# Turning the exponentials of a slots stage in 32x32 blocks on VectorE and through DRAM, where TensorE transposed them

## The chip, the cores and the metric

The kernel runs on one core of a Trainium2 chip. The metric is the device time of one execution in microseconds, from the first to the last instruction of the program. Three runs of the kernel before took 2634.92, 2635.74 and 2637.29 us; their median is 2635.74 us.

## The reference

The kernel computes one transformer layer on float32 data: grouped causal attention with a residual and a layer norm, and then a mixture of experts with soft routing, again with a residual and a layer norm. The change lies in the mixture. Its core, cut to what matters:

```python
x_ln = (x - mean) / jnp.sqrt(var + LN_EPS) * gamma + beta          # B=2, N=2048, D=512
x_n = _l2norm(x_ln, -1) * scale
mu_n = _l2norm(mu, 0)                                              # D, E=16, S=128
logits = jnp.einsum('bnd,des->bnes', x_n, mu_n)
dispatch = jax.nn.softmax(logits, axis=1)                          # over the tokens
combine = jax.nn.softmax(logits.reshape(B, N, E * S), axis=-1)
slot_in = jnp.einsum('bnd,bnes->besd', x_ln, dispatch)
h = jax.nn.gelu(jnp.einsum('besd,edh->besh', slot_in, W1) + b1, approximate=False)
slot_out = jnp.einsum('besh,ehd->besd', h, W2) + b2
out = jnp.einsum('bsd,bns->bnd', slot_out.reshape(B, E * S, D), combine)
```

## The kernel before

The program is a sequence of five stages with a barrier between them: projections, attention, post (output projection and norms), slots, and combine. The change is in slots, which computes `logits`, `slot_in`, `h` and `slot_out`. Every product is made in three passes of float32r halves (`three_passes`, L71 to L75): high times high, high times low, low times high, so each tensor that enters a product is first split, its high half by a copy on ScalarE and its low half by a subtraction on VectorE.

The slots stage works in 32 units, one for each of 2 batches and 16 experts. A unit's logits are a tile of 128 slots by 2048 tokens, held as four groups j = 0 to 3 of 512 tokens (JG = 4), each one PSUM bank. With slots on the partitions the softmax over the tokens is a reduction along the row. The product for `slot_in` however contracts over tokens, so it wants the exponentials with tokens on the partitions: they have to be turned. Per unit:

- **logits(j)** on TensorE (L1347 on): 12 matmuls of 512 columns per group into `ps_l`.
- **copy(j)** on ScalarE (L1469) scales them into `logit`; the SP queue stores all four groups at once to DRAM (`store_logits`, L1313, 1 MB) for the combine stage.
- **maximum(j)** and **largest(j)** on VectorE (L1577, L1593): the row's maximum, whose negative goes into the exponential's bias after the fourth group (L1580, L1582), and a running maximum `most` per token.
- **exp(j)** on ScalarE (L1479) writes `ex`, of which there are two, one for even and one for odd units, and sums the row.
- **transpose(j)** on TensorE (L1371): four 128x128 transposes against an identity into one of two banks of `ps_t`. **split_hi(j)** (ScalarE, L1488) and **split_lo(j)** (VectorE, L1608) make `eT_hi` and `eT_lo` from that bank; of each there are two, for even and odd groups.
- **product(j)** on TensorE: 12 matmuls of 512 columns on `eT_hi`, `eT_lo` and the token rows `xl_hi`, `xl_lo`.
- then, one unit at a time through one bank `ps_e`: **slot_in** (ScalarE, L1497), its transpose (`slot_in_t`, L1396), its split (L1503, L1614), **hidden** (12 matmuls of 128 columns), **gelu** (L1509, L1513), **hidden_lo** (L1618), **slot_out** (3 matmuls), **bias** (L1623), and the split and store of the result (L1519, L1627, L1327, L1329).

The units are pipelined by hand. Each engine has a list of parts with a lag; `walk` runs i from 0 up and emits, in the list's order, each part for unit i minus its lag. So in one round TensorE makes the logits of unit n, the products of unit n-1 and the hidden layer of unit n-2. Engines execute strictly in this written order, and a part that waits for a semaphore holds everything behind it on its engine. TensorE's list:

```python
walk([(1, logits(0)), (3, slot_in_t), (1, logits(1)), (1, logits(2)), (3, hidden),
      (2, transpose(0)), (1, logits(3)), (2, transpose(1)), (3, slot_out), (2, product(0)), (2, transpose(2)),
      (2, product(1)), (2, transpose(3)), (2, product(2)), (1, largest_t), (2, product(3)), (2, largest_rows)])
```

The SP queue issues nearly all DMAs of the stage in one order as well: per round the next expert's `mu` (L1291), the logits (L1313), the expert's weights (L1319, L1320, L1323) and the slot results. Once per batch it loads the token rows: `xT` (L1299) for the logits and `xl` (L1308, 16 tiles) for the products. GpSimd only makes the identity in this stage.

## Time and profile before

| | |
|---|---|
| median of three runs | 2635.74 us |
| the profiled execution, its own time | 2634.77 us |
| its span, first to last instruction | 2633.1 us |
| mean granted TensorE clock | 0.972 of full speed |
| TensorE busy in the span | 2519.9 us (96%) |
| VectorE busy | 1673.7 us (64%) |
| ScalarE busy | 1444.5 us (55%) |
| GpSimd busy | 1099.3 us (42%) |
| slots stage, first to last instruction | about 1352 to 2241 us of the span |
| DMA moved in the whole span | 304.37 MB, 116 GB/s on average |

TensorE is busy nearly throughout. A busy time of matmuls counts them from start to modelled end, and they overlap, so what a matmul costs is read from one start to the next. Idle time of an engine costs nothing unless something that ends last waits for it. The views used below are the page of the profile, its table of instruction groups, the instructions in order of time on one engine, the busy time of each engine in chosen stretches, and the DMA issues with their time from issue to landing.

### The profile page before, as it was taken

What the parts mean: (1) busy time and instruction counts of PE and PEld (TensorE: products, weight loads), DVE (VectorE), ACT (ScalarE), POOL (GpSimd) and SP (SyncE); (2) the same over time, 40 slices, a digit from 0 to 9 for tenths busy, and PEclk for the clock granted to TensorE, in tenths of its full rate; (3) what the DMA queues carried; (4) which work ended last, traced back from release to release, by engine and by line L of the source; (5) the groups of instructions that cost most, each with busy time, mean ns of one, the idle gap of its engine ahead of it and who ended that gap; (6) DMA issues with size and microseconds to landing.
All of it is one profiled execution on the core that took longest, in us unless ns stands there. A gap on an engine that the chain in (4) does not pass through costs nothing. (4 is left out here: it accounts for less than half of the span.)

```text
span 2633.1 us, 39463 instructions
## 1 busy us (share of the span) xinstructions
PE 2519.9 (96%) x13730; PEld 1774.6 (67%) x13730; DVE 1673.7 (64%) x3601; ACT 1444.5 (55%) x2780; POOL 1099.3 (42%) x657
## 2 busy tenths in 40 slices
PE   8989999999999999996969999999999998799998
PEld 7865555555555555544747888887888887688886
DVE  3348887878787877835965444456444444577776
ACT  3214566666566666664865555566555554454453
POOL 4304868677677777686930000000000000355553
PEclk9978999999999999998979999999999999899999
DMA  7841121212221121105963323254232322875453
GB/s 245 283 147 36 35 60 38 63 43 55 53 54 50 49 53 47 34 9 189 350 245 116 120 81 120 81 181 147 86 114 90 111 92 81 288 233 150 132 159 102
DMA packets 205063, 304.37 MB, mean 116 GB/s; under 512 B 40225, under 2 KB 86337, under 8 KB 200641
## 3 DMA queue, kind: packets, MB, share of 16 engines
q1 hardware_dynamic: 201296, 294.72, 35.8%
q0 software_dynamic: 1920, 5.25, 0.6%
q8 instruction: 110, 1.80, 0.3%
q10 hardware_dynamic: 1648, 1.88, 0.2%
q14 instruction: 89, 0.72, 0.1%
HBM read 184.83 MB, written 116.42 MB: 114 GB/s over the span
## 5 line engine op out<-in xcount | busy, mean ns | idle before, releaser
L834 ACT ACTIVATE p_probs<-p_ps_s 128x512 f32<-128x512 f32 (+3 forms) x1280 | 597.0, 539 | 340.4 <-PE p_ps_s L766 330.8
L861 DVE TENSOR_REDUCE p_parts<-p_ps_m 128x1 f32<-128x512 f32 x768 | 472.4, 682 | 91.4 <-PE p_ps_m L753 91.0
L722 POOL TENSOR_TENSOR p_added<-p_added,p_probs 128x2048 f32<-128x2048 f32 x112 | 513.7, 4587 | 20.6 <-ACT p_probs L834 8.4
L753 PE MATMUL p_ps_m<-k_m,q 96*128 96x512 f32 (+3 forms) x1280 | 477.0, 403 | 13.2 <-PEq L1878 7.8
L766 PE MATMUL p_ps_s<-q,k_e 98*128 98x512 f32 (+3 forms) x1280 | 450.6, 382 | 2.2 <-ACT p_probs L834 2.2
L1726 POOL MEMSET p_power<- 128x1 f32 x1 | 0.1, 99 | 890.1 <-POOLq L1878 890.1
L753 PEld LDWEIGHTS p_ps_m<-k_m,q 96*128 96x128 f32 x1280 | 242.7, 193 | 187.8 <-DVE p_parts L861 89.8
L766 PEld LDWEIGHTS p_ps_s<-q,k_e 98*128 98x128 f32 x1280 | 238.3, 191 | 135.2 <-issue 56.7
L785 PE MATMUL p_ps_c<-p_probs,v_e 128*32 128x512 f32 (+3 forms) x2560 | 287.5, 540 | 3.7 <-POOL p_probs L707 3.7
L865 DVE CUSTOM_DVE_ANT_0 p_masked<-p_ps_m,p_mask 128x384 f32<-128x384 f32 (+3 forms) x512 | 223.8, 487 | 99.6 <-PE p_ps_m L753 96.3
L1739 POOL TENSOR_TENSOR p_acc<-p_acc,p_lg 128x512 f32<-128x512 f32 x112 | 162.0, 1447 | 154.6 <-ACT p_lg L1791 151.6
L73 PE MATMUL p_ps_l<-p_xT_hi,p_mu_hi 128*128 128x512 f32 x512 | 207.2, 405 | 16.7 <-DVE p_xT_lo L1555 12.0
L73 PE MATMUL p_ps_o<-p_so,p_c_hi 128*128 128x512 f32 x512 | 204.0, 398 | 17.4 <-DVE p_c_lo L1827 17.4
L73 PE MATMUL p_ps_s<-p_xl_hi,p_eT_hi 128*128 128x512 f32 x512 | 209.2, 409 | 5.5 <-DVE p_eT_lo L1608 5.5
L1469 ACT ACTIVATE p_logit<-p_ps_l,p_inv_n 128x512 f32<-128x512 f32 x128 | 87.8, 688 | 217.1 <-PE p_ps_l L75 217.1
L74 PE MATMUL p_ps_o<-p_so,p_c_hi 128*128 128x512 f32 x512 | 203.2, 397 | 0.0
L75 PE MATMUL p_ps_o<-p_so,p_c_lo 128*128 128x512 f32 x512 | 203.0, 397 | 0.0
L74 PE MATMUL p_ps_s<-p_xl_lo,p_eT_hi 128*128 128x512 f32 x512 | 201.8, 394 | 0.0
L75 PE MATMUL p_ps_s<-p_xl_hi,p_eT_lo 128*128 128x512 f32 x512 | 201.7, 394 | 0.0
L74 PE MATMUL p_ps_l<-p_xT_lo,p_mu_hi 128*128 128x512 f32 x512 | 201.5, 393 | 0.0
L75 PE MATMUL p_ps_l<-p_xT_hi,p_mu_lo 128*128 128x512 f32 x512 | 201.1, 393 | 0.0
L1791 ACT ACTIVATE p_lg<-p_lg 128x512 f32<-128x512 f32 x128 | 81.1, 634 | 170.6 <-DVE p_lg L1823 170.2
(179 smaller groups left out, 4523.7 us busy)
## 6 DMA issues: line engine op xcount, KB each, us to landing
logits_t<-p_logit SPq DMA_DIRECT2D x32, 1024.0 KB, 5.0
p_lg<-logits_t SPq DMA_DIRECT2D x128, 256.0 KB, 3.7
q<-q_t SPq DMA_DIRECT2D x96, 256.0 KB, 4.6
p_w_raw<-L_ffn_W_dram SPq DMA_DIRECT2D x64, 256.0 KB, 5.4
p_so<-slot_out SPq DMA_DIRECT2D x32, 512.0 KB, 6.3
p_x<-L_attn_x_dram SPq DMA_DIRECT2D x32, 256.0 KB, 5.6
q_t<-p_f_hi SPq DMA_DIRECT2D x32, 256.0 KB, 5.3
q_t<-p_f_lo SPq DMA_DIRECT2D x32, 256.0 KB, 5.4
```

The lines of the kernel that those rows point to most:

```text
L73: pe.matmul(out, w_hi, m_hi, start=start, stop=False)
L74: pe.matmul(out, w_hi, m_lo, start=False, stop=False)
L75: return pe.matmul(out, w_lo, m_hi, start=False, stop=stop)
L722: pool.tensor_tensor(a[:, :, :], first[:, :, :], probs[s % RING][:, :, :], ALU.add).then_inc(s_add, 1)
L753: pe.matmul(ps_m[:, u % M_BANKS, 0:w], q[0:QROWS, qb, h, bass.ts(t, P)], k_m[:, c * BLK:c * BLK + w], start=True, stop=True).then_inc(s_un ...
L766: pe.matmul(ps_s[:, u % ST_BANKS, q0:BLK], k_e[:, bass.ts(kt, P)], q[:, qb, h, q0:BLK], start=True, stop=True).then_inc(s_score, 1)
L785: mm = pe.matmul(ps_c[part, 0, q0:BLK], v_e[:, kt, :], probs[s % RING][:, h, q0:BLK], start=s == FIRST[n], stop=last)
L834: act.activation(probs[s % RING][:, h, q0:BLK], ps_s[:, u % ST_BANKS, q0:BLK], ACT.Exp).then_inc(s_exp, 1)
L861: dve.tensor_reduce(to, bank, AX.X, ALU.max).then_inc(s_taken, 1)
L865: dve.tensor_tensor_reduce(masked[u % 4][:, 0:w], bank, mask[:, BLK - w:], 1.0, -3.0e38, ALU.add, ALU.max, to).then_inc(s_taken, 1)
L1469: act.activation(logit[:, j, :], ps_l[:, j, :], ACT.Copy, scale=inv_n[:, n % E:n % E + 1]).then_inc(s_cp, 1)
L1739: pool.tensor_tensor(a[:, :], a[:, :], lg[n % U][:, :], ALU.add).then_inc(s_acc, 1)
```

## The change

TensorE no longer transposes the exponentials, and `ps_t` is gone. VectorE turns them instead: `turn(j)` transposes every 32x32 block of `ex[:, j, :]` (128x512) in place of the blocks, into one of two tiles `turned`. That leaves each block in the partition quarter of its slots, and it must go to the quarter of its tokens. DRAM does this: `store_turned(j)` on the SP queue writes the tile to scratch `eT[j]` (256 KB in pieces of 512 bytes), and the GpSimd queue, once that store has landed, reads it back with four DMAs of 64 KB, one for each 32 partitions, into one of two tiles `eT`. The splits then read `eT` from SBUF, with the blocks put in the order of the tiles by their access patterns. The tokens of a group stand in another order than before, and the rows `xl` are loaded in the same new order: four DMAs of 32 partitions for each group where there were four tiles, with one semaphore for the group.

Other things change with it. There is one `ex` instead of two, so exp(j) waits for the previous unit's turn(j). turn(2) and turn(3) reuse the `turned` tiles of turn(0) and turn(1) of the same unit, and wait until those have been stored. The load of a group into `eT[j % 2]` waits for split_lo of the group two before it. The order of the parts is rewritten on TensorE, ScalarE and VectorE; on the SP queue the four stores stand between the store of the logits and the loads of the weights.

```diff
-        ex = [al.sbuf(f"p4_ex{r}", [P, JG, BANK]) for r in range(2)]
+        ex = al.sbuf("p4_ex", [P, JG, BANK])
+        turned = [al.sbuf(f"p4_turned{r}", [P, NQ, BANK // NQ]) for r in range(2)]
+        eT = [al.sbuf(f"p4_eT{r}", [P, NQ, BANK // NQ]) for r in range(2)]
...
-                        for t in tiles(j):
-                            sp.dma_start(xl_lo[:, t, :].bitcast(F32), d["xl"][n // E * NT + t]).then_inc(s_xl[t], 16)
+                        for p in range(NQ):
+                            sp.dma_start(xl_lo[p * QD:(p + 1) * QD, j * TG:(j + 1) * TG, :].bitcast(F32),
+                                         d["xl"][n // E * NT + j * TG + p].rearrange("(t a) c -> a t c", a=QD)).then_inc(s_xl[j], 16)
...
+            def store_turned(j):
+                def part(n):
+                    sp.wait_ge(s_turn, 4 * n + j + 1)
+                    if n > 0:
+                        sp.wait_ge(s_eT[j % 2], 64 * (2 * n - 2 + j // 2 + 1))
+                    sp.dma_start(d["eT"][j].rearrange("p q f -> q p f"), turned[j % 2][:, :, :]).then_inc(o_turn[j % 2], 16)
+                return part
...
-                 + [(1, store_logits)] + [(2, load_weights)] + [(3, store_out)] + [(1, load_rows(j)) for j in range(JG)])
+                 + [(1, store_logits)] + [(1, store_turned(j)) for j in range(JG)] + [(2, load_weights)] + [(3, store_out)] + [(1, load_rows(j)) for j in range(JG)])
...
+            for n in range(UNITS):
+                for j in range(JG):
+                    at = 4 * n + j
+                    pool.wait_ge(o_turn[j % 2], 16 * (2 * n + j // 2 + 1))
+                    if at >= 2:
+                        pool.wait_ge(s_elo, at - 1)
+                    for p in range(NQ):
+                        pool.dma_start(eT[j % 2][p * QD:(p + 1) * QD, :, :], d["eT"][j, p].rearrange("(i a) f -> a i f", a=QD)).then_inc(s_eT[j % 2], 16)
...
-            def transpose(j):
-                def part(n):
-                    pe.wait_ge(s_ex, 4 * n + j + 1)
-                    if 4 * n + j >= 2:
-                        pe.wait_ge(s_elo, 4 * n + j - 1)
-                    for t in range(TG):
-                        mm = pe.transpose(ps_t[:, j % 2, bass.ts(t, P)], ex[n % 2][:, j, bass.ts(t, P)], ident[:, :])
-                    mm.then_inc(s_tr, 1)
-                return part
...
             walk([(1, logits(0)), (3, slot_in_t), (1, logits(1)), (1, logits(2)), (3, hidden),
-                  (2, transpose(0)), (1, logits(3)), (2, transpose(1)), (3, slot_out), (2, product(0)), (2, transpose(2)),
-                  (2, product(1)), (2, transpose(3)), (2, product(2)), (1, largest_t), (2, product(3)), (2, largest_rows)])
+                  (1, logits(3)), (3, slot_out), (2, product(0)), (2, product(1)), (2, product(2)), (1, largest_t),
+                  (2, product(3)), (2, largest_rows)])
...
-                    act.wait_ge(s_tr, 4 * n + j + 1)
+                    act.wait_ge(s_eT[j % 2], 64 * (2 * n + j // 2 + 1))
                     if 4 * n + j >= 2:
                         act.wait_ge(s_prod, 4 * n + j - 1)
-                    act.activation(eT_hi[j % 2][:, :, :], ps_t[:, j % 2, :], ACT.Copy).then_inc(s_ehi, 1)
+                    act.activation(by_quarter(eT_hi[j % 2]), by_tile(eT[j % 2]), ACT.Copy).then_inc(s_ehi, 1)
...
-            walk([(3, slot_in), (2, rows_hi(0, False)), (1, copy(0)), (2, rows_hi(1, False)), (3, slot_in_hi), (1, copy(1)),
+            walk([(3, slot_in), (2, rows_hi(0, False)), (1, copy(0)), (2, rows_hi(1, False)), (3, slot_in_hi), (1, copy(1)), (2, split_hi(0)),
                   (2, rows_hi(2, False)), (1, copy(2)), (3, gelu), (2, rows_hi(3, False)),
-                  (2, split_hi(0)), (1, copy(3)), (2, split_hi(1)), (1, exp(0)), (1, exp(1)), (0, vectors_hi), (0, unit_rows_hi(0)),
-                  (2, split_hi(2)), (1, exp(2)), (1, exp(3)), (0, unit_rows_hi(1)), (3, out_hi), (2, split_hi(3)),
+                  (2, split_hi(1)), (1, copy(3)), (1, exp(0)), (1, exp(1)), (2, split_hi(2)), (1, exp(2)), (1, exp(3)),
+                  (0, vectors_hi), (0, unit_rows_hi(0)), (0, unit_rows_hi(1)), (3, out_hi), (2, split_hi(3)),
...
+            def turn(j):
+                def part(n):
+                    dve.wait_ge(s_ex, 4 * n + j + 1)
+                    if 4 * n + j >= 2:
+                        dve.wait_ge(o_turn[j % 2], 16 * (2 * n + j // 2))
+                    dve.transpose(turned[j % 2].rearrange("p q f -> p (q f)"), ex[:, j, :]).then_inc(s_turn, 1)
+                return part
...
-                  (1, largest(2)), (0, vectors_lo), (0, unit_rows_lo(0)), (2, split_lo(2)), (1, largest(3)), (0, unit_rows_lo(1)), (1, total),
-                  (3, out_lo), (2, split_lo(3)), (1, largest_col), (0, unit_rows_lo(2)), (0, unit_rows_lo(3))]
+                  (1, largest(2)), (1, turn(0)), (1, turn(1)), (2, split_lo(2)), (1, turn(2)), (1, turn(3)), (0, vectors_lo), (0, unit_rows_lo(0)),
+                  (1, largest(3)), (0, unit_rows_lo(1)), (1, total), (3, out_lo), (2, split_lo(3)), (1, largest_col), (0, unit_rows_lo(2)), (0, unit_rows_lo(3))]
```

On VectorE, the second half of a round in steady state, from the maximum over the fourth group to the split of the weights. Before (`p_most` is largest, `p_mu_lo` is vectors_lo, `p_si` bias, `p_so_lo` out_lo, `p_w_lo` weights_lo; the two small operations on `p_col` after `p_most` are total):

```order
L1577 TENSOR_REDUCE p_col<-p_logit 128x1
L1580 TENSOR_REDUCE p_col<-p_col 128x1
L1582 TENSOR_SCALAR p_col<-p_col 128x1
L1608 TENSOR_TENSOR p_eT_lo<-p_ps_t,p_eT_hi 128x512
L1623 TENSOR_TENSOR p_si<-p_ps_e,p_b 128x512
L1593 TENSOR_TENSOR p_most<-p_most,p_logit 128x512
L1561 TENSOR_TENSOR p_mu_lo<-p_mu_raw,p_mu_hi 128x512
L1608 TENSOR_TENSOR p_eT_lo<-p_ps_t,p_eT_hi 128x512
L1593 TENSOR_TENSOR p_most<-p_most,p_logit 128x512
L1601 TENSOR_REDUCE p_col<-p_col 128x1
L1603 RECIPROCAL p_col<-p_col 128x1
L1627 TENSOR_TENSOR p_so_lo<-p_si,p_so_hi 128x512
```

The split of the fourth group, split_lo(3), follows that last row directly. The same stretch now:

```order
L1648 TENSOR_TENSOR p_si<-p_ps_e,p_b 128x512
L1611 TENSOR_TENSOR p_most<-p_most,p_logit 128x512
L1634 STREAM_TRANSPOSE p_turned<-p_ex 128x512 x2
L1626 TENSOR_TENSOR p_eT_lo<-p_eT,p_eT_hi 128x4x4x32
L1634 STREAM_TRANSPOSE p_turned<-p_ex 128x512 x2
L1579 TENSOR_TENSOR p_mu_lo<-p_mu_raw,p_mu_hi 128x512
L1611 TENSOR_TENSOR p_most<-p_most,p_logit 128x512
L1619 TENSOR_REDUCE p_col<-p_col 128x1
L1621 RECIPROCAL p_col<-p_col 128x1
L1652 TENSOR_TENSOR p_so_lo<-p_si,p_so_hi 128x512
L1626 TENSOR_TENSOR p_eT_lo<-p_eT,p_eT_hi 128x4x4x32
```

The four turns have come in around split_lo(2), and split_lo(3), the last row, stands behind all of them. The splits of groups 0 and 1 have moved ahead of this stretch.

On the SP queue, one round before:

```order
L1291 DMA p_mu_raw<-L_ffn_mu_dram 128x4x128
L1313 DMA logits_t<-p_logit 128x2048
L1319 DMA p_w_raw<-L_ffn_W_dram 128x4x128
L1320 DMA p_w_raw<-L_ffn_W_dram 128x512
L1323 DMA p_b<-L_ffn_b_dram 128x512
L1327 DMA slot_out<-p_so_hi 128x512
L1329 DMA slot_out<-p_so_lo 128x512
```

And now:

```order
L1300 DMA p_mu_raw<-L_ffn_mu_dram 128x4x128
L1331 DMA logits_t<-p_logit 128x2048
L1326 DMA turned<-p_turned 128x4x128 x4
L1337 DMA p_w_raw<-L_ffn_W_dram 128x4x128
L1338 DMA p_w_raw<-L_ffn_W_dram 128x512
L1341 DMA p_b<-L_ffn_b_dram 128x512
L1345 DMA slot_out<-p_so_hi 128x512
L1347 DMA slot_out<-p_so_lo 128x512
```

The four stores stand directly behind the 1 MB of logits, and the loads of the weights behind the four stores.

## Rows read from the trace of the kernel before

**Rows 1.** 1600 to 1700 us: length, busy (count) of PE PEld DVE ACT POOL; clock, DMA, GB/s

```profile
1600.00:1700.00 100.00, 100.00 (x504) 83.60 (x503) 47.19 (x88) 55.30 (x102) 0.00 (x0) 1.00 0.33 106
```

**Rows 2.** TensorE in order of time (start, us, instruction), one unit's round

```profile
1602.06 0.62 PE L1371 MATMUL p_ps_t<-p_ident,p_ex 128*128 128x128 f32 x4
...
1605.28 0.60 PE L1371 MATMUL p_ps_t<-p_ident,p_ex 128*128 128x128 f32 x4
...
1615.60 0.39 PE L73 MATMUL p_ps_s<-p_xl_hi,p_eT_hi 128*128 128x512 f32 x1
...
1618.32 0.39 PE L73 MATMUL p_ps_l<-p_xT_hi,p_mu_hi 128*128 128x512 f32 x1
...
1628.27 0.62 PE L1371 MATMUL p_ps_t<-p_ident,p_ex 128*128 128x128 f32 x4
```

**Rows 3.** VectorE in order of time, a block transpose in attention and what follows

```profile
1006.07 0.71 DVE L895 STREAM_TRANSPOSE p_inv<-p_inv_t 128x512 f32<-128x512 f32 x1
1006.71 1.85 DVE L861 TENSOR_REDUCE p_parts<-p_ps_m 128x1 f32<-128x512 f32 x3
```

**Rows 4.** ScalarE in order of time, same round

```profile
1605.48 0.69 ACT L1469 ACTIVATE p_logit<-p_ps_l,p_inv_n 128x512 f32<-128x512 f32 x1 [1.30 <-PE p_ps_l L75]
...
1606.67 1.28 ACT L1479 ACT_TABLE_LOAD   x1
1607.97 0.73 ACT L1479 ACTIVATE p_ex<-p_logit,p_col 128x512 f32<-128x512 f32 x1
...
1608.69 0.71 ACT L1479 ACTIVATE p_ex<-p_logit,p_col 128x512 f32<-128x512 f32 x1
```

**Rows 5.** VectorE in order of time, same round

```profile
1607.11 0.15 DVE L1582 TENSOR_SCALAR p_col<-p_col 128x1 f32<-128x1 f32 x1
1607.18 0.68 DVE L1608 TENSOR_TENSOR p_eT_lo<-p_ps_t,p_eT_hi 128x512 fp32r<-128x512 f32 x1
1607.78 0.68 DVE L1623 TENSOR_TENSOR p_si<-p_ps_e,p_b 128x512 f32<-128x512 f32 x1
...
1611.95 0.16 DVE L1601 TENSOR_REDUCE p_col<-p_col 128x1 f32<-128x4 f32 x1
```

**Rows 6.** The SP queue in order of time, same round

```profile
1606.19 0.32 SPq L1313 DMA_DIRECT2D logits_t<-p_logit  x1
1606.56 0.43 SPq L1319 DMA_DIRECT2D p_w_raw<-L_ffn_W_dram  x1
```

**Rows 7.** The page, DMA issues: count, KB each, us from issue to landing

```profile
logits_t<-p_logit SPq DMA_DIRECT2D x32, 1024.0 KB, 5.0
...
p_w_raw<-L_ffn_W_dram SPq DMA_DIRECT2D x64, 256.0 KB, 5.4
```

**Rows 8.** DMA issues of the first 260 us, same columns

```profile
p_mu<-L_ffn_mu_dram POOLq DMA_DIRECT2D x32, 128.0 KB, 3.2
...
v<-p_v SPq DMA_DIRECT2D x8, 256.0 KB, 2.5
```

**Rows 9.** GpSimd in order of time, four DMAs of the first stage

```profile
36.79 2.13 POOL L187 DMA_DIRECT2D p_mu<-L_ffn_mu_dram  x4 [1.95 <-DMA mu_squares<-p_mu]
```

**Rows 10.** TensorE in order of time, instructions behind its gaps (gap in brackets)

```profile
1340.27 1.01 PE L1075 MATMUL p_ps_t<-p_ident,p_xn 128*128 128x128 f32 x4 [2.27 <-ACT p_xn L1119]
...
1395.04 0.77 PE L73 MATMUL p_ps_s<-p_xl_hi,p_eT_hi 128*128 128x512 f32 x1 [3.31 <-DVE p_eT_lo L1608]
```

**Rows 11.** Such stretches around two gaps; clock is third from the end

```profile
1381.20:1394.80 13.60, 10.52 (x50) 8.49 (x48) 13.60 (x21) 12.13 (x20) 0.00 (x0) 0.99 0.72 265
1394.80:1398.40 3.60, 3.36 (x8) 2.73 (x9) 2.61 (x7) 2.05 (x5) 0.00 (x0) 0.53 1.00 279
...
1336.80:1340.20 3.40, 1.20 (x10) 0.87 (x8) 3.00 (x8) 2.60 (x6) 1.46 (x3) 1.00 0.52 194
1340.20:1346.00 5.80, 2.13 (x8) 1.32 (x8) 1.57 (x3) 5.08 (x12) 3.62 (x7) 0.52 0.72 268
```

**Rows 12.** The SP queue in order of time, the first loads of token rows

```profile
1374.47 8.79 SPq L1308 DMA_DIRECT2D p_xl_lo<-x_ln  x16
```

More of the change, by code:

```diff
@@ L1223 @@
 TG = NT // JG
+QD = 32
+NQ = P // QD
 def slots(nc, sems, mu, W1, b1_t, W2, b2, d):
@@ L1263, in slots @@
         s_log, s_cp, s_most, s_ex, s_max, s_neg = (sem(n) for n in ("logits", "copied", "most", "exp", "max", "negated"))
-        s_sum, s_rs, s_tr, s_ehi, s_elo, s_prod = (sem(n) for n in ("sum", "inverse", "transposed", "e_hi", "e_lo", "product"))
+        s_sum, s_rs, s_turn, s_ehi, s_elo, s_prod = (sem(n) for n in ("sum", "inverse", "turned", "e_hi", "e_lo", "product"))
         s_si, s_sT, s_sThi, s_sTlo = sem("slot_in"), sem("slot_in_t"), sem("slot_in_hi"), sem("slot_in_lo")
@@ L1895, in layer @@
         "inv": scratch("slot_norm", [P, E]),
+        "eT": scratch("turned", [JG, NQ, P, P]),
         "logit": scratch("logits_t", [B * E, P, N]),
```

21 lines of the change are left out of this document (12 added, 9 removed).

## The prediction

> **What bounds the kernel now.** I began with the busy times by stretch. In a hundred microseconds of the slots stage TensorE is never without a matmul in flight, at full granted clock (2.4 GHz), while VectorE is busy 47% and ScalarE 55% of it [rows 1]: TensorE's own work sets the pace. Then TensorE in order of time: from one transpose(0) to the next is 1628.27 - 1602.06 = 26.21 us, which is the period of a unit [rows 2]. Twelve matmuls of 512 columns without transposes take 1618.32 - 1615.60 = 2.72 us, so 0.227 us each; four transposes and twelve such matmuls take 1605.28 - 1602.06 = 3.22 us [rows 2]. Four transposes therefore cost 0.50 us, less than their shown 0.62, since they overlap with what follows and slow it a little.
>
> **Removed from TensorE.** Four groups of 0.50 us are 2.0 us per unit. If nothing else came to bind, the period would fall from 26.21 to 24.2 us, and over 31 periods the kernel by 62 us. The question is what the new route makes late.
>
> **A round of the new kernel.** I count t from the start of logits(0). logits(3) starts 1628.27 - 1618.32 = 9.95 us later [rows 2] and ends at 12.67; slot_out takes 3 x 0.23; the products could start at 13.36, 16.08, 18.80 and 21.52, and the round would end at 24.24.
>
> *ScalarE.* copy(3) began at 1605.48, 0.20 us behind the last matmul of logits(3) [rows 2, 4]: t = 12.87. Now the exponential's table load follows directly: copy 0.6, load 1.28, so exp(0) starts at 14.77; each exp takes 0.72 to the next [rows 4] and its result is there about 0.8 after its start: exp(0) at 15.6, exp(1) at 16.3.
>
> *VectorE.* The negated maximum was done at 1607.26, 1.78 us after copy(3) began [rows 4, 5]: t = 14.65. An operation on 128x512 takes 0.60 us from start to start (1607.18 to 1607.78) [rows 5]. bias and largest(2) follow, to 15.85. The turn itself can be priced: the attention stage has block transposes of this shape, 0.71 us long and 0.64 to the next start [rows 3]. turn(0) runs from 15.85 to 16.5, turn(1) to 17.1, split_lo(2) to 17.7.
>
> The Trainium skill ("VectorE: DVE Perf Modes", The three transpose paths) speaks against the exchange: it has 390 ns for a 128x128 transpose on TensorE and 311 ns on VectorE, says the latter makes 32x32 blocks only, and advises TensorE for 128x128. By its figures, for another type, four would be an estimated 1.24 us a turn; the three turns on the path below would add about 1.8 us per unit to my sum. The row of the same shape has 0.71, and the row decides.
>
> *The stores.* turn(2) overwrites the tile of turn(0) and waits until it is stored. In the kernel before, the 1 MB of logits is issued at 1606.19, 0.71 after copy(3) began [rows 4, 6]: t = 13.58, and lands 5.0 us later [rows 7], at 18.6. The 256 KB behind it on the same queue, issued 0.37 later and landing after 5.4 [rows 6, 7], lands 0.77 after it. The store of turn(0), issued at 16.6, stands in that place: 18.6 + 0.8 = 19.4. Alone, a store of this size and with these short pieces takes 2.5 us [rows 8], which gives 19.1: the lower bound. GpSimd's four reads for group 3 of the unit before (256 KB more) are issued at 13.2 to 15.4 and share the DMA engines; they cost between nothing and another 0.8, and I take 0.4. So turn(2) starts at 19.8, not at 17.7, and turn(3), whose tile lands about 0.6 later, at 20.4, ending at 21.1.
>
> *What is queued behind.* After turn(3) on VectorE come vectors_lo, largest(3), total (two operations 0.19 apart, 0.38) and out_lo, then split_lo(3): 3 x 0.60 + 0.38 + 0.69 = 2.87 us [rows 5], done at 23.95. product(3) waits for it and starts at 24.0 instead of 21.52. That is a **stall of 2.4 us per unit**, and the period is 24.24 + 2.4 = 26.7, against 26.21: 31 x 0.46 = **+14 us**. The 2.0 us gained on TensorE are all given back in this wait.
>
> *The rest of the route* has slack. GpSimd issues 16 DMAs per unit at 0.53 us (2.13 for four) [rows 9], 8.5 of 26.7 us. A load after split_lo(0) (t = 8.2) has been issued by 10.3 and lands, with 3.2 us for such a DMA [rows 8], by 13; split_hi(2) wants it at 16.3. The one for group 3 lands by 18.5; split_hi(3) wants it before split_lo(3) at 23. ex is single now, but exp(0) waits for a turn of the round before. The weights are now loaded behind the four stores, issued at about 22 and landing about 27 to 28, which is where ScalarE waits, ahead of slot_in; slot_in_t is due at 26.7 + 2.7 = 29.4, and slot_in needs some 2 us after the weights. That cover is thin, and I count nothing for it. The splits read SBUF instead of PSUM at the same length within 0.05 us.
>
> **The clock.** A stall of 2.4 us is not only its length. Behind gaps of 3.31 and of 2.27 us the granted clock stood at half, 1.2 GHz; the stretches ahead of them show 0.99 and 1.00, those behind 0.53 and 0.52. The stretch of 3.6 us at 0.53 has 8 matmuls in it where 15 would fit: about 1.6 us lost [rows 10, 11]. A gap of 2.4 lies among those that were followed by a fall, but in the 2.27 case mostly short transposes ran before and after, so I take a fall in half the units. product(3) and the next logits run in it, and both are on the path; part of the slow stretch may lie in the gap, so 1.5 us each: 15 x 1.5 = **+23 us** (bounds 0 and 31 x 1.6 = 50).
>
> **Once only.** At the start the rows xl were issued from 1374.47 on, 0.55 us each [rows 12]; now they stand behind four stores, of which the last waits for turn(3), itself behind two landings after a 1 MB store: about 7 us later, of which about 5 reach the first product. At the change of batch the same order costs 1 to 3 us, and the first mu_lo of a round now comes behind turn(3). I take **+8 us** together (3 to 15).
>
> **Sum.** 2634.8 + 14 + 23 + 8 = 2680 us, against the profiled execution's own time, which is 1.0 us under the median of 2635.7; I forecast **2680**, 1.7% slower.
>
> **Rivals.**
>
> *A: the hold on turn(2) is hidden, and the kernel is faster.* If the store of turn(0) landed before 17.7, so 1.1 us after its issue, turn(3) would end at 19.05, split_lo(3) at 21.9, and the stall be 0.4 us, a sixth of the smallest gap that I have before a fall. Period 24.7: 31 x -1.5 = -47, with +8: **about 2596**. The turning point is where the stall equals the gain of 2.0 us, split_lo(3) at 23.5, hence turn(2) at 19.35. For it speaks that VectorE is half idle; against it that no DMA of this size lands in less than 2 us in this part and that 1 MB is ahead of it. 0.08.
>
> *B: even.* The ends of my bounds: stores land as if alone (19.1), the clock never falls: stall 1.8, period 26.0, 31 x -0.2 + 8: **about 2637**. 0.12.
>
> *C: the clock falls in every unit.* 31 x (0.46 + 1.6) + 8 = 72: **about 2707**. The Trainium skill ("TensorE: Matmul & The Clock Gate", HAM oscillation) describes this, a loop with a wait in each turn that is throttled anew every time. The trace has gaps of this size only singly, so it can neither show nor exclude it. 0.17.
>
> *D: the loads become the bound.* Around one unit go split_lo(0), load, split_hi(2), split_lo(2), load of the next unit's group 0: two landings and two splits, room for about 11 us per landing at this period. If the mix of stores, software-issued reads and weights took 13 us, the period would be 30 and the time near 2750. The late weights could act likewise through slot_in. 0.06.
>
> *E: the change does not do what it says* (transposes still on TensorE) is excluded by the order of the instructions.
>
> **Chances.** My own case, with its unknown parts (contention 0 to 0.8 us, falls 5 to 25 of 31, once-only 3 to 15) gives 2650 to 2700 and has 0.57. The range that leaves out at most two in ten takes in B's and C's values with 5 to 8 us around them: 2632 to 2715. A difference of 0.2%, about 5 us, is what a measurement of this kernel can tell from none. Faster by more: case A and a part of B, 0.12. Within it: part of B, 0.06. Slower: 0.82.
>
> **What would show it.** In the changed profile: a block transpose of 128x512 at 0.71 us on VectorE, four per unit; before the third of them a VectorE idle of about 2 us released by the DMA of `turned`; TensorE idle before the first matmul of product(3), about 2.4 us per unit, released by split_lo(3); periods of 26.7 us and, where the clock fell, 28; mean clock under 0.972. I am wrong if TensorE's idle sits before another instruction, if it is under 1 us, or if ScalarE waits for `eT` before the split of group 2 or 3.

## The result, and the profile after

The changed kernel takes 2713.8 us, the median of four runs (2712.1 to 2717.6), beside 2635.3 us for the kernel before on the same chip (four runs, 2633.9 to 2637.3). The ratio is 1.0299, with a 95% interval of 1.0281 to 1.0317: **78.5 us slower**. The prediction was 2680, range 2632 to 2715: its sign is right, its size (+44 of +78) a little over half, and the result lies 1.2 us inside the upper end of the range.

| | before | after |
|---|---|---|
| the profiled execution, its own time | 2634.8 | 2717.6 |
| its span | 2633.1 | 2715.9 |
| mean granted TensorE clock | 0.972 | 0.953 |
| TensorE busy | 2519.9 | 2502.4 |
| VectorE busy | 1673.7 | 1747.3 |
| GpSimd busy | 1099.3 | 1379.0 |
| DMA moved | 304.37 MB | 371.51 MB |

The profiled execution is the slowest of the four, so it shows 82.8 us where the medians differ by 78.5. The same hundred microseconds of the slots stage as in [rows 1], after:

```profile
1600.00:1700.00 100.00, 91.62 (x423) 75.02 (x422) 54.77 (x102) 53.18 (x97) 34.52 (x64) 0.98 0.54 176
```

TensorE, which had no gap there, is now idle 8.4 us in a hundred, and the DMA engines carry 176 GB/s instead of 106. VectorE is still little over half busy: neither resource is full. So the time is in a wait, and the next view to read is the order of time. Here is VectorE in one ordinary round, the counterpart of [rows 5] (start, us, engine, line, instruction, count, and in brackets the idle time before it and what ended it):

```profile
1662.22 0.68 DVE L1611 TENSOR_TENSOR p_most<-p_most,p_logit 128x512 f32<-128x512 f32 x1
1662.82 1.35 DVE L1634 STREAM_TRANSPOSE p_turned<-p_ex 128x512 f32<-128x512 f32 x2
1664.10 0.65 DVE L1626 TENSOR_TENSOR p_eT_lo<-p_eT,p_eT_hi 128x512 fp32r<-128x512 f32 x1
1666.58 1.54 DVE L1634 STREAM_TRANSPOSE p_turned<-p_ex 128x512 f32<-128x512 f32 x2 [1.83 <-DMA turned<-p_turned]
...
1669.47 0.67 DVE L1652 TENSOR_TENSOR p_so_lo<-p_si,p_so_hi 128x512 fp32r<-128x512 f32 x1
1670.06 0.68 DVE L1626 TENSOR_TENSOR p_eT_lo<-p_eT,p_eT_hi 128x512 fp32r<-128x512 f32 x1
```

And TensorE in the same round (the counterpart of [rows 2]): the first matmul of logits(0), the first of product(3), and the first of the next round.

```profile
1646.91 0.39 PE L73 MATMUL p_ps_l<-p_xT_hi,p_mu_hi 128*128 128x512 f32 x1
...
1670.80 0.50 PE L73 MATMUL p_ps_s<-p_xl_hi,p_eT_hi 128*128 128x512 f32 x1 [2.10 <-DVE p_eT_lo L1626]
...
1673.67 0.39 PE L73 MATMUL p_ps_l<-p_xT_hi,p_mu_hi 128*128 128x512 f32 x1
```

Read the two together. turn(2) starts at 1666.58 - 1646.91 = 19.67 us into the round, held 1.83 us by the landing of a store of `turned`. split_lo(3), queued behind it, runs at 1670.06, and product(3) has waited 2.10 us for it. The round is 1673.67 - 1646.91 = 26.76 us, where TensorE's work alone would make 24.24. Grouped over the slots stage (count, busy us, mean ns of one, idle before them and its releasers), this chain is the whole picture:

```profile
L73 PE MATMUL p_ps_s<-p_xl_hi,p_eT_hi 128*128 128x512 f32 x498 | 210.3, 422 | 82.2 <-DVE p_eT_lo L1626 81.9
...
L1634 DVE STREAM_TRANSPOSE p_turned<-p_ex 128x512 f32<-128x512 f32 x128 | 88.6, 710 | 70.4 <-DMA turned<-p_turned 67.3 <-ACT p_ex L1497 0.8
...
L1626 DVE TENSOR_TENSOR p_eT_lo<-p_eT,p_eT_hi 128x512 fp32r<-128x512 f32 x126 | 85.4, 678 | 9.1 <-ACT p_eT_hi L1506 9.1
...
L1506 ACT ACTIVATE p_eT_hi<-p_eT 128x512 fp32r<-128x512 f32 x126 | 78.4, 622 | 4.2 <-DMA p_eT<-turned 3.0 <-PE p_ps_s L75 1.0
...
L1543 ACT ACTIVATE p_w_hi<-p_w_raw 128x512 fp32r<-128x512 f32 x31 | 19.6, 632 | 226.0 <-DMA p_w_raw<-L_ffn_W_dram 226.0
```

ScalarE waits 3.0 us in all for a block to come back from DRAM: the loads, which the change adds on GpSimd, are not the trouble. The 226 us for the weights look worse and cost nothing in an ordinary round, because nothing stands behind that wait until slot_in. In the unit behind the first two they did cost: ScalarE got the weights late, slot_in followed them, and TensorE waited 2.63 us for it.

```profile
1426.38 0.63 ACT L1543 ACTIVATE p_w_hi<-p_w_raw 128x512 fp32r<-128x512 f32 x1 [8.54 <-DMA p_w_raw<-L_ffn_W_dram]
...
1428.16 1.12 PE L1413 MATMUL p_ps_e<-p_ident,p_si 128*128 128x128 f32 x4 [2.63 <-ACT p_si L1515]
```

Keep this wait in mind for the third experiment. The DMA issues (count, KB each, us from issue to landing), against [rows 7]:

```profile
turned<-p_turned SPq DMA_DIRECT2D x128, 256.0 KB, 3.0
p_eT<-turned POOLq DMA_DIRECT2D x512, 64.0 KB, 3.1
```

**Where the 82.8 us are.** I take each round's length as the time from one first matmul of logits(0) to the next. Before, all but three of these lengths are 26.21 or 26.22 us (the first holds two units). After:

| rounds | before | after | excess |
|---|---|---|---|
| the first two units | 48.2 | 63.6 | +15.4 |
| the unit behind them | 26.2 | 32.6 | +6.4 |
| last unit of batch 1 | 29.3 | 37.7 | +8.4 |
| first products of batch 2 | 35.9 | 44.3 | +8.3 |
| 26 others, the common part | 26.21 | 26.7 | 26 x 0.5 = +13.0 |
| 7 of these, at 28.2 | | +1.5 each | +10.5 |
| 5 of these, at 29.0 to 31.0 | | +2.3 to +4.3 | +18.5 |
| the rest (end of the stage and after) | | | +2.3 |

In the seven rounds of 28.2 us the granted clock fell to 1.2 GHz behind the stall. Stretches around the one at 1918.9 (clock is third from the end):

```profile
1918.00:1920.00 2.00, 1.12 (x3) 0.96 (x4) 0.83 (x2) 0.00 (x0) 0.62 (x2) 0.80 0.97 279
1920.00:1922.00 2.00, 2.00 (x6) 1.54 (x5) 0.00 (x0) 0.00 (x0) 1.55 (x3) 0.50 0.84 256
```

The lower row is the same work at half clock: 6 matmuls in 2 us, where rows at full clock have 10 to 12 (a matmul on an edge is counted with its stretch), or 0.43 us from one start to the next where full clock has 0.23. In the rounds of 29 to 31 us the hold itself is longer; in the one that began at 2113.67 turn(2) was held 3.34 us and started 4.5 us after the issue of the store instead of 3.0. But the clock fell in all five of them too. The stretch behind the wait of that round:

```profile
2139.50:2143.50 4.00, 4.00 (x10) 3.09 (x10) 0.00 (x0) 0.65 (x2) 2.17 (x4) 0.50 1.00 303
```

The five rounds have 47 matmuls at a start-to-start time of 0.43 us, so about 9.4 of their 18.5 us are the clock; their waits for p_eT_lo (2.5 to 4.2 us) are together 6.6 us longer than in five ordinary rounds. In all, the clock fell in 12 of these 26 rounds and took about 20 us.

### The profile page after: what moved, and what is told of

It reads as the page before. It is cut to its first block and busy times, and to the rows that moved or that the text cites. A ratio compares the mean times of both kernels' runs of the same rounds, so it can differ in the third digit from the quotient of the medians.

```text
span 2715.9 us, 39461 instructions
## 1 busy us (share of the span) xinstructions
PE 2502.4 (92%) x13218; PEld 1745.3 (64%) x13218; DVE 1747.3 (64%) x3729; ACT 1445.6 (53%) x2780; POOL 1379.0 (51%) x1169
## 2 busy tenths in 40 slices
DMA packets 289034, 371.51 MB, mean 137 GB/s; under 512 B 50464, under 2 KB 162112, under 8 KB 284608
## 5 line engine op out<-in xcount | busy, mean ns | idle before, releaser
L1369 POOL DMA_DIRECT2D p_eT<-turned x512 | 277.9, 550 | 670.6 <-DVE p_eT_lo L1626 444.0
L73 PE MATMUL p_ps_s<-p_xl_hi,p_eT_hi 128*128 128x512 f32 x512 | 216.0, 422 | 82.2 <-DVE p_eT_lo L1626 81.9
L74 PE MATMUL p_ps_s<-p_xl_lo,p_eT_hi 128*128 128x512 f32 x512 | 211.8, 414 | 0.0
L75 PE MATMUL p_ps_s<-p_xl_hi,p_eT_lo 128*128 128x512 f32 x512 | 211.1, 412 | 0.0
L73 PEld LDWEIGHTS p_ps_s<-p_xl_hi,p_eT_hi 128*128 128x128 f32 x512 | 103.9, 203 | 117.2 <-DVE p_eT_lo L1626 77.0
```

The lines of the kernel that those rows point to most:

```text
L73: pe.matmul(out, w_hi, m_hi, start=start, stop=False)
L74: pe.matmul(out, w_hi, m_lo, start=False, stop=False)
L75: return pe.matmul(out, w_lo, m_hi, start=False, stop=stop)
L1369: pool.dma_start(eT[j % 2][p * QD:(p + 1) * QD, :, :], d["eT"][j, p].rearrange("(i a) f -> a i f", a=QD)).then_inc(s_eT[j % 2], 16)
```

## The experiments

Ratios are to the kernel before, run on the same chip in the same session; its medians there were 2634.3 to 2635.8 us. "Round" is the most frequent round length.

### e1_four_turned: no store to wait for

```diff
-        ex = al.sbuf("p4_ex", [P, JG, BANK])
-        turned = [... for r in range(2)]
+        ex = al.sbuf("p4_ex", [P, 2, BANK])
+        turned = [... for r in range(JG)]
-                    if 4 * n + j >= 2:
-                        dve.wait_ge(o_turn[j % 2], 16 * (2 * n + j // 2))
+                    if n > 0:
+                        dve.wait_ge(o_turn[j], 16 * n)
```

> The edit gives `turned` four tiles with a semaphore each, and takes the space from `ex` (two groups in place of four): no turn waits any more for a store of its own unit. My theory: turn(2) is held only by the landing of turn(0)'s store, and that hold is the stall of 2.1 us ahead of product(3). Then turn(2) and turn(3) start about 1.8 us earlier, split_lo(3) is done before product(2) ends, the stall is under 0.3 us, the steady round is 24.3 to 24.9 us instead of 26.7, and since the queue of TensorE has no gap left most falls of the clock go: 2640 to 2665 us. Rival 1, VectorE is the bound by the sheer work it took on: the stall stays at over 1.5 us and the time within 0.4% of 2714. Rival 2, the blocks come back too late through DRAM (the gpsimd loads): p_eT_hi on ScalarE begins to wait for DMA, the stall stays. Rival 3, with shorter rounds the weights land after the round's end: slot_in is late, and a new wait of 0.5 to 2 us at slot_in_t takes its place: 2665 to 2700.

Measured: 2623.6 us, ratio 0.9953 [0.9938, 0.9968], so **90 us less than the changed kernel and 0.5% faster than the kernel before**. The round is 24.77 us. In the stretch 1600 to 1700 VectorE's wait for `turned` is gone, and TensorE's weight loads wait 0.6 us at most for p_eT_lo. The hold is the cause of the stall; VectorE's work (rival 1) and the way through DRAM (rival 2) are not. I had the round right and the sum too high: with the stall, the rounds of 28.2 and those of 29 to 31 went altogether, which is 29 us by the table above. Rival 3 is there in traces only: in three rounds (26.1, 25.6 and 25.2 us) slot_in_t waited 1.1, 0.7 and 0.2 us for slot_in.

### e2_logits_behind: what makes the store take 3 us

```diff
-                 + [(1, store_logits)] + [(1, store_turned(j)) for j in range(JG)]
+                 + [(1, store_turned(0)), (1, store_turned(1)), (1, store_logits), (1, store_turned(2)), (1, store_turned(3))]
```

> The edit issues the 1 MB store of the logits behind the stores of turn(0) and turn(1) instead of ahead of them. My theory: the store of turn(0) takes 3.0 us because it shares the 16 DMA engines with the 1 MB that was issued 3 us before it; alone it would land 0.4 to 0.8 us sooner, turn(2) starts that much earlier, and the round shortens by as much: 2695 to 2705 us. The rounds of 29 to 31 us, in which the store of the logits took 6.1 us and that of turn(0) 4.1, should lose most of their excess, for another 10 to 20 us: 2680 to 2700 in all. Rival: 3.0 us is what a store of 256 KB takes with nothing beside it: no change within 0.3%.

Measured: 2677.4 us, ratio 1.0153 [1.0136, 1.0170], 36 us less than the changed kernel. SP and VectorE in order of time:

```profile
1602.82 1.00 SPq L1326 DMA_DIRECT2D turned<-p_turned  x2
```

```profile
1605.10 1.50 DVE L1634 STREAM_TRANSPOSE p_turned<-p_ex 128x512 f32<-128x512 f32 x2 [1.09 <-DMA turned<-p_turned]
```

turn(2) starts 2.28 us after the issue, where with the 1 MB ahead it was 3.02 (1663.56 to 1666.58). The stall falls from 2.1 to 1.3 and the round from 26.7 to 26.0. And the long rounds are nearly gone: the five of 29.0 to 31.0 are now 26.0, 27.2, 27.9, 26.2 and 26.6. So the megabyte in flight ahead of the small store set 0.7 us of the common hold of 1.8 and most of its outliers. The falls of the clock went with them: over the same 26 rounds there is one, behind a wait of 1.87 us, where the changed kernel had 12. Why the outliers fall where they do stays open.

### e3_split_ahead: the stall taken away, the hold left

```diff
-                  (2, split_hi(1)), ... (1, exp(3)),
-                  (0, vectors_hi), ... (3, out_hi), (2, split_hi(3)),
+                  (2, split_hi(1)), ... (1, exp(3)), (2, split_hi(3)),
+                  (0, vectors_hi), ... (3, out_hi),
...
-  (2, split_lo(2)), (1, turn(2)), (1, turn(3)), ... (3, out_lo), (2, split_lo(3)), (1, largest_col)
+  (2, split_lo(2)), (2, split_lo(3)), (1, turn(2)), (1, turn(3)), ... (3, out_lo), (1, largest_col)
```

> The edit leaves the hold on turn(2) as it is, but puts split_hi(3) ahead of vectors_hi and out_hi on ScalarE and split_lo(3) ahead of turn(2) on VectorE, so that product(3) no longer waits behind the held turn. My theory: the wait for p_eT_lo ahead of product(3) goes, but turn(2) and turn(3) end 0.7 us later, the weights are issued behind their stores and land some 28 us after the round's start, now 3 to 4 us into the next round: slot_in is late, slot_in_t on TensorE waits 2 to 3 us for it, and little is won: 2690 to 2720 us. Rival, that late weights don't matter: 2640 to 2665 us.

Measured: 2752.1 us, ratio 1.0436 [1.0421, 1.0452]: **38 us more** than the changed kernel, worse than I expected, by the mechanism that I expected. Most rounds are 28.4 to 31.0 us. ScalarE, then TensorE, one round on (it began at 1487.02):

```profile
1491.69 0.63 ACT L1543 ACTIVATE p_w_hi<-p_w_raw 128x512 fp32r<-128x512 f32 x1 [8.18 <-DMA p_w_raw<-L_ffn_W_dram]
...
1492.75 0.67 ACT L1515 ACTIVATE p_si<-p_ps_s,p_col 128x512 f32<-128x512 f32 x1
```

```profile
1493.47 1.12 PE L1413 MATMUL p_ps_e<-p_ident,p_si 128*128 128x128 f32 x4 [3.57 <-ACT p_si L1515]
```

The wait for p_eT_lo is gone and another has taken its place. The weights, issued behind four stores, land 4.7 us into the next round; slot_in stands behind their split, and TensorE waits 3.57 us for it. That is the wait of 226 us that cost nothing a moment ago. What made it worse than my estimate is the clock, which now falls behind this gap in round after round:

```profile
1490.00:1493.50 3.50, 0.03 (x1) 0.03 (x1) 0.62 (x2) 1.80 (x4) 0.00 (x0) 0.78 0.83 297
1493.50:1499.00 5.50, 5.50 (x16) 4.49 (x17) 2.55 (x5) 1.09 (x2) 0.00 (x0) 0.52 0.04 12
```

24.33 + 3.57 leaves 2.7 us of this round of 30.6, of which 9 matmuls at half clock are 1.8. This is the picture of my rival C, in a version of the kernel in which the gap is mostly 3.4 to 4.2 us and not 2.1; even here a few rounds kept their clock, one of them behind a gap of 3.58 us. The Trainium skill ("TensorE: Matmul & The Clock Gate", HAM oscillation) describes such a loop, throttled anew in every turn; this trace agrees in most rounds, that of the changed kernel, with its falls in 12 of 26, only in part.

### e4_ahead_weights and e11_weights_early: the two together, and the control

e4 is e3 with one more part moved on the SP queue; e11 has this alone.

```diff
-                 + [(1, store_logits)] + ... + [(2, load_weights)] + [(3, store_out)] + ...
+                 + [(2, load_weights), (1, store_logits)] + ... + [(2, load_bias)] + [(3, store_out)] + ...
```

> As the kernel with split_lo(3) ahead of turn(2), and w1 and w2 of the next unit are issued ahead of the store of the logits (b2 stays behind the stores). My theory: now neither the hold nor the weights stand before TensorE; the round is 24.3 to 24.9 us, the falls of the clock are mostly gone, and what remains beside the kernel before is the once-only part (about 40 us at the start, the change of batch and the end): 2635 to 2665 us, with the hold of 1.8 us still there on VectorE. Rival 1, VectorE's work is the bound: the stall comes back at p_mu_lo or p_eT_lo, and the round stays over 26 us.

> The changed kernel with w1 and w2 issued ahead of the store of the logits, and nothing else: the control to e3 (split ahead alone, 2752 us) and e4 (both, 2614 us). My theory: in a round of 26.7 us the weights land some 0.6 us after the round's end and are hidden under logits(0), so loading them early wins only what slot_in waits in the few disturbed rounds, and perhaps, with 512 KB fewer on the engines behind the turned stores, a little of the excess of the rounds of 29 to 31 us: 2695 to 2712 us; the steady round stays at 26.7 us and the stall ahead of product(3) at 2.1 us. Rival: if the late weights were part of the stall, the round would fall to under 26.3 us and the time to under 2690.

Measured: e4 2614.3 us, ratio 0.9919 [0.9904, 0.9934]; e11 2707.4 us, ratio 1.0284 [1.0267, 1.0300]. Alone, the early weights give 6 us by the medians, but e11's own runs spread from 2696.7 to 2712.3 and the two intervals overlap, so this gain isn't clear of the noise. In e11's trace the unit behind the first two takes 27.1 us instead of 32.6, without TensorE's wait for slot_in, and the ordinary round is still 26.7. Behind the moved split they are worth 138 us. In e4, 25 of the 29 rounds behind the first two units are 24.33 or 24.34 us; the others are the two at the change of batch, the one between them (24.40) and one of 25.42. The stretch of [rows 1], in e4:

```profile
1600.00:1700.00 100.00, 99.25 (x469) 82.48 (x468) 59.12 (x110) 58.67 (x106) 34.67 (x64) 1.00 0.58 190
```

TensorE is again all but without a gap, at full clock, with two tiles of `turned` as before: turn(2) now stands behind split_lo(3), which has to wait for product(1) anyway, and the store lands meanwhile. The round of 24.33 us is the 24.24 that I had worked out for TensorE's work. So taking the transposes off TensorE does give its 2 us per unit, and the change had given them back in one place of VectorE's order, with late weights as the next wait behind it.

### e5_largest_ahead: a wait that moves

```diff
-  (2, split_lo(2)), (2, split_lo(3)), (1, turn(2)), (1, turn(3)), (0, vectors_lo), (0, unit_rows_lo(0)), (1, largest(3)),
+  (2, split_lo(2)), (1, largest(3)), (2, split_lo(3)), (1, turn(2)), (1, turn(3)), (0, vectors_lo), (0, unit_rows_lo(0)),
```

> As e4_ahead_weights (2614 us), and largest(3) stands on VectorE between split_lo(2) and split_lo(3), where e4 idles 2 us, instead of behind turn(2), turn(3) and vectors_lo. It concerns the last unit of a batch alone, where TensorE transposes the maxima (largest_t) between product(2) and product(3) and in e4 waits 8.2 us for largest(3). My theory: this wait goes, 2605 to 2609 us, and no steady round changes (24.33 us). Rival: largest_t waits for something else there (the copies of the logits, the change of batch on DMA), and the time stays within 2 us of e4.

Measured: 2614.6 us, ratio 0.9925 [0.9910, 0.9940]: nothing, as the rival's number said. TensorE's wait of 8.2 us for p_most is gone, and the next round opens with

```profile
1777.99 0.76 PE L73 MATMUL p_ps_l<-p_xT_hi,p_mu_hi 128*128 128x512 f32 x1 [8.93 <-DVE p_m_col L1668]
```

The maxima are turned sooner but reduced (largest_col) as late as ever, behind the split of the next batch's rows. My theory named the wait and missed what was late next.

### e6_rows_by_128, e7_rows_first, e8_with_four: a load on four engines

```diff
-                        for p in range(NQ):
-                            sp.dma_start(xl_lo[p * QD:(p + 1) * QD, j * TG:(j + 1) * TG, :].bitcast(F32),
-                                         d["xl"][n // E * NT + j * TG + p].rearrange("(t a) c -> a t c", a=QD)).then_inc(s_xl[j], 16)
+                        for t in range(TG):
+                            sp.dma_start(xl_lo[:, j * TG + t, :].bitcast(F32),
+                                         d["xl"][n // E * NT + j * TG:n // E * NT + (j + 1) * TG, t * QD:(t + 1) * QD, :]).then_inc(s_xl[j], 16)
```

> As e5_largest_ahead, and the rows p_xl_lo, whose order in SBUF the change permuted, are loaded by 16 transfers to all 128 partitions (256 KB each, four runs of 32 rows of DRAM) instead of 16 transfers to 32 partitions each; same bytes, same number of issues, same places. My theory: the transfers to 32 partitions move 230 GB/s at a full share of the 16 DMA engines, where the rows of the kernel before moved at 380 to 400; to 128 partitions they run at 380 again, a group of 1 MB lands in 2.7 us instead of 4.7, and the last of the four groups at the start lands 8 us earlier: 8 to 12 us less than e5. Rival: the permuted order in DRAM (runs of 32 rows) is what costs, and the rate stays at 230 GB/s: within 2 us of e5.

Measured: 2659.0 us, ratio 1.0092 [1.0075, 1.0109], 44 us **more** than e5. Both theories are wrong about it, as one row says (DMA share and GB/s are last):

```profile
1400.00:1405.00 5.00, 0.00 (x0) 0.00 (x0) 0.00 (x0) 0.00 (x0) 0.00 (x0) 0.50 0.26 102
```

A quarter of the engines' time at a quarter of the rate: this form, whose outermost dimension in DRAM is 4, behaves as if it ran on four of the sixteen DMA engines. The Trainium skill ("DMA: Bandwidth & Descriptors", Why a DMA increments its semaphore by 16 and not by 1) says that a DMA gets the largest number of engines up to 16 that divides the slowest dimension other than 1 of both its sides, here 4 and 128. That makes four, and the trace agrees with its share of 0.26.

e7 adds, to e6, the issue of the first rows ahead of all stores, and e8 adds to e7 the four tiles of e1.

> As e6_rows_by_128, and the first batch's rows are issued ahead of the first store of logits and the four stores of turned blocks, which hold them back from 1374.5 (kernel before) to 1381.7 us. My theory: at the start TensorE waits for these rows and nothing else, so they come 5 to 7 us earlier and the kernel is 4 to 7 us shorter than e6. Rival: the stores of the turned blocks and their loads now share the engines with 4 MB of rows, split_hi(0) waits for them instead of for the rows: less than 2 us.

> As e7_rows_first, with the four turned tiles of e1_four_turned. My theory: in e4 the hold on turn(2) has no cost left, it lies under split_lo(3)'s wait for product(1), and the steady round of 24.33 us is TensorE's own work (107 matmuls of 512 columns): no change, within 3 us. Rival: the hold still costs something at the start and the change of batch, where transfers are slow: 3 to 8 us less.

Measured: e7 2650.8 us, ratio 1.0063 [1.0048, 1.0078]; e8 2639.3 us, ratio 1.0019 [1.0010, 1.0028]. e7 is 8.2 us under e6, more than the 4 to 7 of my theory, and its start looks otherwise than I had thought: with rows this slow, SP took 28 us to issue eleven of their loads, the stores of `turned` stood behind them, and in e7 one turn on VectorE was held 34.54 us, with vectors_lo behind it; TensorE waited 41.0 us for p_mu_lo. With four tiles that wait is 6.4 us. e8 is 11.5 us under e7. So e8's rival holds in kind, with more than its 3 to 8 us: the hold that costs nothing in a steady round does cost where a transfer is slow.

### e9_rows_in_order: why the start was dear

```diff
-                sp.dma_start(d["xl"][n, :, :], xl[n % R4][:, :]).then_inc(o_xl[n % R4], 16)
+                for t in range(TG):
+                    sp.dma_start(d["xl"][n // TG * TG + t, n % TG * QD:(n % TG + 1) * QD, :], xl[n % R4][t * QD:(t + 1) * QD, :]).then_inc(o_xl[n % R4], 16)
...
-                        for p in range(NQ):
-                            sp.dma_start(xl_lo[p * QD:(p + 1) * QD, j * TG:(j + 1) * TG, :].bitcast(F32), ...
+                        for t in tiles(j):
+                            sp.dma_start(xl_lo[:, t, :].bitcast(F32), d["xl"][n // E * NT + t]).then_inc(s_xl[j], 16)
```

> The changed kernel with one thing altered: the stage ahead (post) stores each tile of x_ln with 4 transfers of 32 partitions into the permuted order, and the slots stage loads it with 16 transfers of 256 KB to 128 partitions each, one contiguous tile of DRAM each, as the kernel before does. e6_rows_by_128 had fallen to 102 GB/s at a quarter of the engines' share, because its transfers had an outermost dimension of 4. My theory: a load to 32 partitions is what holds the changed kernel at 229 GB/s with all 16 engines busy, and this is most of the once-only cost of about 40 us: now 380 GB/s, the rows of the start land 8 us sooner (the first two units 8 to 12 us shorter in all), the change of batch is 4 to 8 us shorter, and the stage ahead does not notice its 96 further stores: 2694 to 2703 us. Rival: loads and rows are not what the start waits for (the stall is on the turned blocks): within 0.3% of 2714.

Measured: 2704.2 us, ratio 1.0260 [1.0243, 1.0277], 10 us less than the changed kernel, 1 us short of the 2703 that my theory ended at. ScalarE's splits of the first rows, in the changed kernel and then in e9:

```profile
1389.02 2.20 ACT L1476 ACTIVATE p_xl_hi<-p_xl_lo 128x512 fp32r<-128x512 f32 x4 [11.74 <-DMA p_xl_lo<-x_ln]
1393.91 2.19 ACT L1476 ACTIVATE p_xl_hi<-p_xl_lo 128x512 fp32r<-128x512 f32 x4 [2.69 <-DMA p_xl_lo<-x_ln]
```

```profile
1393.15 2.20 ACT L1474 ACTIVATE p_xl_hi<-p_xl_lo 128x512 fp32r<-128x512 f32 x4 [11.42 <-DMA p_xl_lo<-x_ln]
1395.60 2.19 ACT L1474 ACTIVATE p_xl_hi<-p_xl_lo 128x512 fp32r<-128x512 f32 x4 [0.25 <-DMA p_xl_lo<-x_ln]
```

The second group comes 2.45 us after the first instead of 4.89. The same five microseconds of the span in both kernels, again the changed kernel first:

```profile
1395.00:1400.00 5.00, 0.00 (x0) 0.00 (x0) 2.87 (x6) 2.56 (x6) 0.00 (x0) 0.70 1.07 226
```

```profile
1395.00:1400.00 5.00, 2.03 (x9) 1.33 (x8) 4.78 (x9) 4.22 (x9) 0.00 (x0) 1.00 1.05 380
```

Both have the DMA engines at a full share; to 32 partitions they move 226 GB/s, to 128 they move 380. The first two units and the one behind them take 85.3 us together instead of 96.2, and the first products of batch 2 40.2 instead of 44.3: 15 us in all. That the medians differ by 10 only is in part that the first matmul of the stage comes 4.5 us later in this trace (1363.61 against 1359.07); e3, whose stage ahead is unchanged, has 1362.92, so whether the 96 further stores cost something there isn't shown. The Trainium skill ("SBUF — State Buffer", Door 1: The DMA port swizzle) says that partitions 0 to 31 reach 8 of the 16 ports, and that the bandwidth depends on how many ports are reached. An estimate by that rule is half the rate; 226 of 380 is 0.59, so the trace agrees in direction and not quite in size.

### e10_best and e12_change_of_batch: all of it together

e10 is e5 with e9's stores and loads, the first rows issued first, e1's four tiles, and largest_col ahead of vectors_lo. e12 moves, in e10, the next batch's rows forward:

```diff
-  + [(1, store_turned(j)) for j in range(JG)] + [(2, load_bias)] + [(3, store_out)] + [(1, load_rows(j, False)) for j in range(JG)]
+  (1, store_turned(0)), (1, store_turned(1)), (1, load_rows(0, False)), (1, store_turned(2)), (1, load_rows(1, False)),
+  (1, store_turned(3)), (1, load_rows(2, False)), (2, load_bias), (3, store_out), (1, load_rows(3, False))
...
-  (3, slot_in), (2, rows_hi(0, False)), (1, copy(0)), (2, rows_hi(1, False)), (3, slot_in_hi), (1, copy(1)),
+  (3, slot_in), (1, copy(0)), (3, slot_in_hi), (2, rows_hi(0, False)), (1, copy(1)),
```

> All that helped in one kernel: split_hi(3) and split_lo(3) ahead, weights early, largest(3) and largest_col ahead of what they waited behind, rows stored in order as in e9_rows_in_order and loaded first at the start, four turned tiles. My theory: steady rounds of 24.33 us as in e4; against e5 (2614.6 us) 8 to 12 us less at the start from the rate of the rows and 4 to 6 from issuing them first, 4 to 8 less at the change of batch, 3 to 6 less from largest_col: 2582 to 2599 us, so 1.4 to 2% faster than the kernel before. Rival: the start is bound by what stands on TensorE and ScalarE there, and the transfers only shift: 2600 to 2612 us.

> As e10_best (2590 us), and at the change of batch the rows of the next batch are issued between the stores of the turned blocks, as soon as their group is free, instead of behind all of the round's transfers, and on ScalarE and VectorE slot_in_hi and copy(0) stand ahead of the first group of rows. In e10 the unit in which the batch changes takes 39.5 us, with 5.1 us of waiting for p_siT_lo and 3.5 for p_h_lo behind the rows, which land 6 us late. My theory: that unit falls to 29 to 33 us, nothing else changes: 2580 to 2585 us. Rival: VectorE has to split 16 tiles of rows (9.6 us) beside its 18 us of work of a round, so the unit is bound by VectorE at about 28 us plus the order's own waits and gains under 4 us.

Measured: e10 2590.1 us, ratio 0.9832 [0.9817, 0.9846]; e12 **2579.8 us, ratio 0.9793 [0.9779, 0.9807]**, 2.1% faster than the kernel before. Of e10's 24.5 us against e5, the first two units give 18.3 (64.2 to 45.9) and the end of batch 1 with the round behind it 7.0 (61.6 to 54.7). Its four edits were not run apart on top of e5, so how much each of them gave isn't shown. In e12 the unit in which the batch changes takes 28.6 us instead of 39.5. Both came out at the good end of what I expected. Over the slots stage of e12 the two groups that made the picture of the changed kernel read:

```profile
L73 PE MATMUL p_ps_s<-p_xl_hi,p_eT_hi 128*128 128x512 f32 x512 | 200.7, 392 | 5.4 <-DVE p_eT_lo L1628 5.4
...
L1636 DVE STREAM_TRANSPOSE p_turned<-p_ex 128x512 f32<-128x512 f32 x128 | 84.9, 697 | 0.8 <-ACT p_ex L1499 0.8
```

## Why the prediction was right, and where it fell short

**Right: the gain on TensorE and its loss.** The free round was taken as 24.24 us; e4 and e12 have rounds of 24.33.

**Right: the hold.** turn(2) was put at 19.8, it came at 19.67; a stall of 2.4 us was forecast, 2.10 measured; a round of 26.7 forecast, 26.7 measured. e1 takes the hold away and e3 and e4 take what stands behind it away, and both show that nothing else holds product(3). The turning point, turn(2) at 19.35, holds as well: in e2 it starts at 18.9 (1631.06 - 1612.19) and the round of 26.0 is just under the 26.2 of before; of the 42 us by which e2 is still slower, 39 lie in the first three units, the end of batch 1 and the change of batch.

**Right: the price of the block transpose.** 0.71 us from the attention stage's row was 710 ns on average in the slots stage.

**Right, in part by luck: the clock.** 1.5 us for a fall was measured as 1.5, and of my 15 rounds with a fall 12 came in the 26 ordinary rounds and two more in those of the once-only part, about 20 us in the 26 where the sum had 23. But 15 was a guess at half, between bounds of 0 and 31. Behind waits of 1.9 to 2.2 us the clock fell in 7 of 21 rounds, and five of the twelve falls came behind longer waits, of 2.5 to 4.2 us, that I hadn't foreseen. The length of the wait alone does not settle it either: in e11 three waits of 3.0 to 3.4 us were followed by no fall. The longest of them, and the stretch around it:

```profile
2128.78 0.50 PE L73 MATMUL p_ps_s<-p_xl_hi,p_eT_hi 128*128 128x512 f32 x1 [3.43 <-DVE p_eT_lo L1629]
```

```profile
2128.00:2132.00 4.00, 3.22 (x14) 2.67 (x15) 1.93 (x4) 0.15 (x1) 2.17 (x4) 1.00 1.06 336
```

What decides between a fall and none stays open.

**Wrong: the once-only part.** "I take +8 us together (3 to 15)" was the step that failed. It measured 38.5 us in four places, and 41 with the end. I had priced little more than the later issue of the rows behind the stores, at 7 us; they were issued 5.2 us later (1379.68 against 1374.47). Missed were, first, that a load to 32 partitions moves 226 GB/s and not the 380 to 396 of the kernel before (e9: 15 us by the lengths of the rounds, 10 by the medians). Second, the last unit of a batch waits on TensorE for largest(3), which the change had put behind turn(3) (+8.4). There turn(2) was held 6.16 us, and with four tiles (e1) the same unit takes 32.3 us instead of 37.7; e5 shows that moving largest(3) alone gains nothing, and that largest_col has to move with it is argued from e5's next wait, since e10 moves it together with other things. Third, the late weights, which the prediction gave a thin cover: in the unit behind the first two TensorE waited 2.63 us for slot_in, and with early weights (e11) that unit is 5.5 us shorter. The diff showed the first two, a new shape of DMA and a new place in VectorE's order, and I counted neither.

**Wrong: no term for uneven rounds.** I took one landing time for all rounds. Five rounds in which the store landed late cost 18.5 us. About 9.4 of these are the clock, counted above, and 9.1 are the longer waits and what goes with them, for which the sum had nothing. e2 shows that the megabyte ahead of the store is what lets them grow.

**The thin cover.** "That cover is thin, and I count nothing for it" was true for the ordinary rounds of the change as made, but not for the unit behind the first two, and it was decisive for the obvious mend: e3 went to 2752 us through just this wait.

So, with the clock of all rounds in one term, 13 + 19.9 + 9.1 + 38.5 + 2.3 = 82.8 us stand where the sum had 14 + 23 + 8 = 45. The once-only part is 30.5 us too small, the missing term for longer holds 9.1 and the rest 2.3; the clock and the common part are about 4 too large. That 2713.8 lies within the range is luck: my own case ended at 2700, and the range reached 2715 only for rival C, a fall of the clock in every unit, which did not happen.

## What to carry to other kernels

When a part that waits for a transfer is put into an engine's fixed order, the price is not the wait but what stands behind it: ask which queued part is due first, put that one ahead, and then ask what its new place makes late. A wait that costs next to nothing (here the weights, 226 us of it) is a debt that falls due as soon as the round gets shorter. And a DMA of the same bytes is not the same DMA: look at how many partitions and how long an outermost dimension it has, and read the GB/s beside the share of the engines.
